# The mixer's between-chunks product as three fp32r passes of high and low parts, with signed decay sums kept once and their turns two slots later

## What is computed

```
proj = einsum('bsd,ed->bse', x, in_proj_w)          # gate, x part, B and C, dt
A_cum = cumsum(A_dt)                                # decay sums in chunks of 128
Y_diag = einsum('bzlhn,bzshn,bhzls,bzshp->bzlhp', Cc, Bc, L, xch)
decay_states = exp(A_cum[..., -1:] - A_cum)
states = einsum('bzlhn,bhzl,bzlhp->bzhpn', Bc, decay_states, xch)
Y_off = einsum('bzlhn,bzhpn,bhzl->bzlhp', Cc, prev, exp(A_cum))
Y = Y_diag + Y_off + hs * D
```

## Time and profile before

| | |
|---|---|
| median of 3 runs | 2562.69 us (2562.52 to 2564.77) |
| the profiled execution | 2562.39 us |
| its span, first to last instruction | 2560.7 us |
| busy: PE, PEld | 2473.7 us (97%), 2009.8 us (78%) |
| busy: DVE, ACT, POOL | 1827.8 us (71%), 1486.1 us (58%), 1540.6 us (60%) |
| mean granted TensorE clock | 0.990 |
| the chain that ended last | PE 56%, DVE 2%, POOL 1%, issue 1% |

### The profile page before, as it was taken

One profiled execution on the slowest core, in us unless ns is written; L12 is line 12 of the kernel. 1 busy time (PEld: TensorE's weight loads), 2 busy tenths in 40 slices (PEclk: granted clock), 3 DMA queues, 4 the chain that ended last, 5 costly groups with the idle time before them and its releaser, 6 DMA issues.

```text
span 2560.7 us, 53900 instructions
## 1 busy us (share of the span) xinstructions
PE 2473.7 (97%) x19326; PEld 2009.8 (78%) x19326; DVE 1827.8 (71%) x2688; ACT 1486.1 (58%) x3410; POOL 1540.6 (60%) x1495
## 2 busy tenths in 40 slices
PE   5999999999999888999999999999999999999989
PEld 4878788788887677787888788778878877887777
DVE  5776766767767778668778678587687786785864
ACT  3535535445354465666765775676667657756721
POOL 1654656546556332667767677686677676676810
PEclk8999999999999989999999999999999999999999
DMA  3230230312303024323322222222232223222111
GB/s 101 43 84 29 69 79 22 83 43 49 82 26 71 29 74 160 115 67 115 101 75 83 100 92 75 94 102 96 67 113 94 76 88 104 83 82 94 59 39 49
DMA packets 93549, 199.00 MB, mean 78 GB/s; under 512 B 11248, under 2 KB 19440, under 8 KB 93296
## 3 DMA queue, kind: packets, MB, share of 16 engines
q1 hardware_dynamic: 93296, 195.64, 24.8%
HBM read 184.46 MB, written 11.14 MB: 76 GB/s over the span
## 4 chain that ended last, share of the span: by engine, by line
PE 56%; DVE 2%; POOL 1%; issue 1%; DMA 0%; ACT 0%; SPq 0%; POOLq 0%; DVEq 0%; ACTq 0%
PE proj L210 13%; PE proj L212 12%; PE proj L211 12%; PE core_y L1633 5%; PE core_o L1639 3%; PE turned L245 1%; PE mx_decay L210 1%; PE mx_decay L212 1%; PE mx_decay L211 1%; PE core_y L212 1%; PE core_y L210 1%; PE core_y L211 1%; PE turned L1663 1%; PE mx_normed L1663 1%; PE mx_normed L245 1%; PE core_o L1673 1%
## 5 line engine op out<-in xcount | busy, mean ns | idle before, releaser
L210 PE MATMUL proj<-slab_hi,XTL 128*128 128x512 f32 x816 | 348.3, 427 | 1.0 <-DVE mx_gate L1853 0.4
L193 DVE TENSOR_TENSOR slab_lo<-slab_raw,slab_hi 128x512 fp32r<-128x512 f32 (+2 forms) x256 | 239.2, 946 | 118.7 <-ACT slab_hi L184 117.5
L212 PE MATMUL proj<-slab_hi,XTH 128*128 128x512 f32 x816 | 320.0, 392 | 0.0
L211 PE MATMUL proj<-slab_lo,XTH 128*128 128x512 f32 x816 | 319.0, 391 | 0.0
L210 PE MATMUL proj<-XTH,slab_lo 128*128 128x512 f32 x716 | 289.9, 405 | 25.0 <-PEq L81 7.4
L212 PE MATMUL proj<-XTH,slab_hi 128*128 128x512 f32 x716 | 282.6, 395 | 0.0
L211 PE MATMUL proj<-XTL,slab_hi 128*128 128x512 f32 x716 | 282.4, 394 | 0.0
L210 PE MATMUL proj<-slab_hi,mx_otl 128*128 128x512 f32 x576 | 240.5, 418 | 3.0 <-DVE mx_otl L259 3.0
L1921 POOL TENSOR_TENSOR mx_gate<-mx_gate,mx_hd 128x512 f32<-128x512 f32 x128 | 167.4, 1308 | 102.7 <-DVE mx_hd L1824 91.9
L904 POOL TENSOR_TENSOR at_ropeA<-at_ropeA,at_ropeB 128x512 f32<-128x512 f32 x80 | 110.5, 1381 | 195.0 <-DVE at_ropeB L840 195.0
L212 PE MATMUL proj<-slab_hi,mx_oth 128*128 128x512 f32 x576 | 227.7, 395 | 0.0
(11 more groups left out here) (415 smaller groups left out, 6672.7 us busy)
## 6 DMA issues: line engine op xcount, KB each, us to landing
mx_g_all<-sums SPq DMA_DIRECT2D x128, 512.0 KB, 3.7
at_g_all<-sums SPq DMA_DIRECT2D x64, 256.0 KB, 8.1
slab_raw<-in_w_gate SPq DMA_DIRECT2D x64, 256.0 KB, 2.9
slab_raw<-in_w_out SPq DMA_DIRECT2D x64, 256.0 KB, 2.8
slab_raw<-in_w_x SPq DMA_DIRECT2D x60, 256.0 KB, 4.7
slab_raw<-in_w_q SPq DMA_DIRECT2D x32, 256.0 KB, 2.8
slab_raw<-in_w_g SPq DMA_DIRECT2D x32, 256.0 KB, 2.9
slab_raw<-in_w_o SPq DMA_DIRECT2D x32, 256.0 KB, 5.3
```

The source lines that it names most:

```text
L193: op = nc.vector.tensor_tensor(K.SL[par][:, c, 0:width], K.RAW[c][:, 0:width], hi, ALU.subtract)
L210: nc.tensor.matmul(to[:, 0:bh.shape[-1]], al, bh, start=(c == 0), stop=False)
L211: nc.tensor.matmul(to[:, 0:bh.shape[-1]], ah, bl, start=False, stop=False)
L212: mm = nc.tensor.matmul(to[:, 0:bh.shape[-1]], ah, bh, start=False, stop=(c == KC - 1))
```

## The change

It has four parts.

1. The between-chunks product is made like the units: CBO is kept as a high part (ScalarE's copy at slot 8 of even halves, as before, but rounded) and a low part (VectorE, new), XD as a high part (ScalarE, new) and a low part (VectorE, new), and TensorE does low by high, high by low and high by high in fp32r. The new operations on XD stand in slots r = 1, 4, 8 and 10 (`XD_AT`), after that slot's decays and before its gate. TensorE waits for the low part (`mx_xdl`) where it waited for GpSimd's XD. There is one XD and one low part, where XD had two buffers; GpSimd's next XD waits for the low part of the last.
2. The decay sums are kept once, negated for the first four tiles and as they are for the last four; from_start is made in two operations instead of one.
3. The turns of G and of RR, and the copies out of them, stand at slots 24 and 28 of the middle phase instead of 22 and 26.
4. The small tensors of the last router lie in a free part of another tensor; its operations are the same.

```diff
@@ -923,12 +923,10 @@
     S = K.S
     av, vv, tt, xs = (S[f"{n}_1"] for n in ("rt_a", "rt_v", "rt_T", "rt_x"))
     N, U = K.slab, K.unit
-    def sb(name, shape, dt=F32):
-        return mem.enter_context(nc.sbuf_tensor(f"rt1_{name}", shape, dt))
     scT = room[:, 0:2, :].rearrange("p t n -> p (t n)")
     LG, E, R1, R2 = (room[:, 2 + i, :].rearrange("p (t e) -> p t e", t=NT) for i in range(4))
-    top, top2 = sb("top", [P, NT, 8]), sb("top2", [P, NT, 8])
-    se, rs, ws = sb("sum", [P, NT]), sb("rsum", [P, NT]), sb("wsum", [P, NT])
+    top, top2 = (room[:, 7, i * NT * 8:(i + 1) * NT * 8].rearrange("p (t k) -> p t k", t=NT) for i in range(2))
+    se, rs, ws = (room[:, 7, (16 + i) * NT:(17 + i) * NT] for i in range(3))
     banks = [K.PT, K.PO]
 
     @block.sync
@@ -1081,7 +1079,7 @@
     STEPS = 9
     DT_READY, G_READY, R_READY = 8, 10, 11
     first_block = INTER // P
-    SCAN_AT, Q_AT, G_AT, R_AT, STORE_AT = 14, 18, 22, 26, 15
+    SCAN_AT, Q_AT, G_AT, R_AT, STORE_AT = 14, 18, 24, 28, 15
 
     @block.sync
     def _(sp):
@@ -1359,13 +1357,14 @@
                 for i, bank in enumerate((K.PT, K.PD)):
                     src = bank[:, :].rearrange("p (t h) -> p t h", t=4)
                     act.wait_ge(tt, HEAD + 2 + i + 1)
-                    nc.scalar.activation(less[:, 4 * i:4 * i + 4, :], src, ACT.Copy, scale=-1.0)
-                    nc.scalar.activation(upto[:, 4 * i:4 * i + 4, :], src, ACT.Copy).then_inc(cc, 1)
+                    nc.scalar.activation(signed[:, 4 * i:4 * i + 4, :], src, ACT.Copy, scale=2.0 * i - 1.0).then_inc(cc, 1)
             if u == R_AT:
                 act.wait_ge(tt, HEAD + 5)
                 nc.scalar.activation(to_end[:, :, :].rearrange("p b h -> p (b h)"), K.PT[:, :], ACT.Exp, scale=-1.0).then_inc(cc, 1)
                 act.wait_ge(cc, HEAD + 4)
-                nc.scalar.activation(from_start[:, :, :], upto[:, 1::2, :], ACT.Exp).then_inc(cc, 1)
+                for i in range(2):
+                    nc.scalar.activation(from_start[:, 2 * i:2 * i + 2, :], signed[:, 4 * i + 1:4 * i + 4:2, :], ACT.Exp,
+                                         scale=2.0 * i - 1.0).then_inc(cc, 1)
 
     @block.vector
     def _(dve):
@@ -1519,6 +1518,7 @@
     S = K.S
     N, U, T = K.slab, K.unit, K.tile
     SLOTS, OFF = 24, 8
+    XD_AT = [1, 4, 8, 10]
 
     units = [("x", i) for i in range(8)] + GATE_OUT
     split = {2 * c: [(1, c)] for c in range(4)}
@@ -1551,12 +1551,13 @@
         ACC = sb("ACC", [P, NT, HID])
         BT, CT = sb("BT", [P, TOK]), sb("CT", [P, TOK])
         CBM = sb("CBM", [P, NT, P])
-        CBO = sb("CBO", [P, NB, P])
+        CBH, CBL = sb("CBO_hi", [P, NB, P], F32R), sb("CBO_lo", [P, NB, P], F32R)
         acc = [sb(f"acc{i}", [P, HALF]) for i in range(3)]
         th = sb("th", [P, HALF])
         M = [sb(f"m{i}", [P, 4, P]) for i in range(4)]
         XCH = [sb(f"xch{i}", [P, HH1, P1]) for i in range(2)]
-        XD = [sb(f"xd{i}", [P, HH1, P1]) for i in range(2)]
+        XD, XDL = sb("xd", [P, HH1, P1]), sb("xd_lo", [P, HH1, P1], F32R)
+        XDH = [sb(f"xd_hi{i}", [P, HH1, P1], F32R) for i in range(2)]
         TO = sb("to", [P, HW])
         HD = [sb(f"hd{i}", [P, HW]) for i in range(2)]
         acc.append(HD[1])
@@ -1634,9 +1635,13 @@
                                               XCH[t % 2][:, h, :], start=True, stop=True)
                 mm.then_inc(S["mx_y"], 1)
                 if t % 2:
-                    pe.wait_ge(S["mx_xd"], HEAD + NB * q + b + 1)
+                    pe.wait_ge(S["mx_xdl"], HEAD + NB * q + b + 1)
                     pe.wait_ge(S["mx_to"], HEAD + NB * q + b)
-                    nc.tensor.matmul(K.PO[:, :], CBO[:, b, :], XD[b % 2][:, :, :], start=True, stop=True).then_inc(S["mx_pof"], 1)
+                    if b == 0:
+                        pe.wait_ge(S["mx_cbl"], HEAD + q // 2 + 1)
+                    nc.tensor.matmul(K.PO[:, :], CBL[:, b, :], XDH[b % 2][:, :, :], start=True, stop=False)
+                    nc.tensor.matmul(K.PO[:, :], CBH[:, b, :], XDL[:, :, :], start=False, stop=False)
+                    nc.tensor.matmul(K.PO[:, :], CBH[:, b, :], XDH[b % 2][:, :, :], start=False, stop=True).then_inc(S["mx_pof"], 1)
 
             def half(g, s, last):
                 q = 2 * g + s
@@ -1742,7 +1747,7 @@
                                              TB[u % 2][:, :].rearrange("p (t n) -> p t n", t=4), ACT.Copy).then_inc(S["mx_hs"], 1)
                     if s == 0 and sl == 8:
                         act.wait_ge(S["mx_a"], HEAD + 3 * g + 3)
-                        nc.scalar.activation(CBO[:, :, :].rearrange("p b n -> p (b n)"), K.PO[:, :], ACT.Copy).then_inc(S["mx_bt"], 1)
+                        nc.scalar.activation(CBH[:, :, :].rearrange("p b n -> p (b n)"), K.PO[:, :], ACT.Copy).then_inc(S["mx_bt"], 1)
                     if r in SCORE1:
                         t = SCORE1.index(r)
                         if t < 4:
@@ -1757,14 +1762,19 @@
                             for h in range(4):
                                 at, head = PD[k][:, h * P:(h + 1) * P], ds(HH1 * q + 4 * k + h, 1)
                                 if t < 4:
-                                    ex = nc.scalar.activation(at, GB[t % 4][:, 4 * k + h, :], ACT.Exp, bias=less[:, t, head])
+                                    ex = nc.scalar.activation(at, GB[t % 4][:, 4 * k + h, :], ACT.Exp, bias=signed[:, t, head])
                                 else:
-                                    rl = nc.scalar.activation(at, GB[t % 4][:, 4 * k + h, :], ACT.Relu, bias=upto[:, t, head], scale=-1.0)
+                                    rl = nc.scalar.activation(at, GB[t % 4][:, 4 * k + h, :], ACT.Relu, bias=signed[:, t, head], scale=-1.0)
                             if t >= 4:
                                 rl.then_inc(S["mx_rl"], 1)
                                 act.wait_ge(S["mx_rl"], HEAD + 8 * q + 2 * (t - 4) + k + 1)
                                 ex = nc.scalar.activation(PD[k][:, :], PD[k][:, :], ACT.Exp, scale=-1.0)
                             ex.then_inc(S["mx_e"], 1)
+                    if r in XD_AT:
+                        b = XD_AT.index(r)
+                        act.wait_ge(S["mx_xd"], HEAD + NB * q + b + 1)
+                        act.wait_ge(S["mx_pof"], HEAD + NB * q + b - 1)
+                        nc.scalar.activation(XDH[b % 2][:, :, :], XD[:, :, :], ACT.Copy).then_inc(S["mx_xdh"], 1)
                     if last and s == 1:
                         for t in XT_AT.get(sl, ()):
                             tile_xt_hi(nc, K, act, "d", t, XTB[t])
@@ -1829,6 +1839,10 @@
                                 dve.wait_ge(S["mx_cm"], HEAD + NT * (q + 1))
                             nc.vector.tensor_tensor(TO[:, :].rearrange("p (h n) -> p h n", h=HH1), K.PO[:, :].rearrange("p (h n) -> p h n", h=HH1),
                                                     bc(from_start[:, b, ds(HH1 * q, HH1)], [P, HH1, P1]), ALU.mult).then_inc(S["mx_to"], 1)
+                    if s == 0 and sl == 8:
+                        dve.wait_ge(S["mx_bt"], HEAD + g + 1)
+                        nc.vector.tensor_tensor(CBL[:, :, :].rearrange("p b n -> p (b n)"), K.PO[:, :],
+                                                CBH[:, :, :].rearrange("p b n -> p (b n)").bitcast(F32), ALU.subtract).then_inc(S["mx_cbl"], 1)
                     if r in SCORE1:
                         t = SCORE1.index(r)
                         for k in range(2):
@@ -1845,6 +1859,11 @@
                         dve.wait_ge(S["mx_cm"], HEAD + NT * q + sl - 1)
                         a = acc[(sl - 1) % 4][:, :]
                         nc.vector.scalar_tensor_tensor(a, TH[(sl - 1) % 2][:, :], 1.0, a, ALU.add, ALU.mult).then_inc(S["mx_cm"], 1)
+                    if r in XD_AT:
+                        b = XD_AT.index(r)
+                        dve.wait_ge(S["mx_xdh"], HEAD + NB * q + b + 1)
+                        dve.wait_ge(S["mx_pof"], HEAD + NB * q + b)
+                        nc.vector.tensor_tensor(XDL[:, :, :], XD[:, :, :], XDH[b % 2][:, :, :].bitcast(F32), ALU.subtract).then_inc(S["mx_xdl"], 1)
                     if last and s == 1:
                         for t in XT_AT.get(sl, ()):
                             tile_xt_lo(nc, K, dve, "d", t, XTB[t])
@@ -1938,9 +1957,9 @@
                         hs = HS[:, t, :].rearrange("p (h n) -> p h n", h=HH1)
                         if t % 2 == 0:
                             pool.wait_ge(S["mx_xc"], HEAD + NT * q + t + 1)
-                            pool.wait_ge(S["mx_pof"], HEAD + NB * q + b - 1)
+                            pool.wait_ge(S["mx_xdl"], HEAD + NB * q + b)
                             alone(pool)
-                            nc.gpsimd.tensor_tensor(XD[b % 2][:, :, :], XCH[t % 2][:, :, :], bc(to_end[:, b, heads], [P, HH1, P1]),
+                            nc.gpsimd.tensor_tensor(XD[:, :, :], XCH[t % 2][:, :, :], bc(to_end[:, b, heads], [P, HH1, P1]),
```

12 lines of the change are left out of this document (6 added, 6 removed).

## The result

The changed kernel takes 2568.14 us (median of 20 runs, 2562.57 to 2574.02), the kernel before 2563.72 us beside it: ratio 1.0017, 95% interval 1.001 to 1.0023. A second series gave 1.0011 (1.0002 to 1.002). It is slower by some 3 to 4.4 us; neither interval holds 1. In the series of the experiments two executions lay far off all others (9113 us, one of run 1, and 3080 us, one of the kernel before) and are left out of every ratio. The profiled execution took 2571.65 us with a span of 2569.6.

A forecast was written before the change was run, and what follows sets the result against it. TensorE was taken to bound the mixer, idling only 3.4 us there. Terms -10.9 + 15.8 + 0.5 + 0.9 - 1.1 = +5.2 us on the profiled 2562.4 gave 2567.6, stated as 2567.5 us, range 2557 to 2577.

The forecast's parts named there:

- What the passes give back: Mixer's between-chunks products: three fp32r passes make each 0.17 us shorter, 64 in all, 10.9 us.
- Rival 3: Mixer: the three passes are no shorter, 10.9 us lost but 8.2 us less waiting; 2570 us, slower; chance 0.05.
- The wait at t = 7 for yb(6): Mixer: TensorE's product waits for VectorE's late yb(6), 0.91 us in even and 1.06 in odd halves, 15.8 us.
- about 0.25 of that comes back: Even halves, slot r = 11: VectorE regains 0.25 us at the slab's first low part, leaving yb(6) 0.67 us late.
- so it slips in between at 1185.33 to 1185.93: Odd halves: VectorE's new subtraction fits between two GpSimd operations, taking 0.60 us; yb(6) comes 0.55 us late.
- the second rival: Mixer: the r = 10 subtraction waits out a whole GpSimd operation, 1.30 us; 2577 to 2585 us, slower; chance 0.13.
- Rival 1: Mixer: VectorE makes up the time and no wait arises; 2551 us, faster; chance 0.13.
- Middle phase: VectorE's waits for ScalarE fall from 1.09 to about 0.6 and 2.10 to about 1.65 us; 1.1 us less.
- Rival 4: Middle phase: TensorE's 3.60 us wait was on the path, gain about 4.9 us; 2563.7 us, no change; chance 0.07.
- First group: Mixer's first group: CBO's low part delays the products of t = 0, adding 0.5 us.
- Tail: After the mixer's last half: one more VectorE subtraction and the later copy add about 0.9 us.

The follow-up runs named there:

- run 1: The changed kernel with VectorE doing yb(6) ahead of slot r = 11's slab_lo and otl: ratio 0.9984 to the kernel before, mixer 1365.9 us.
- run 5: The changed kernel with yb(6) first in slot r = 11 and yb(7), TO(3) first in slot r = 12 on VectorE: ratio 0.9974, 2557.2 us.
- run 10: run 5 plus, in odd halves but the last, VectorE's scalings X(3) and X(4) moved to the ends of slots r = 14 and 15: ratio 0.9942, 2549.5 us.
- third order: VectorE's order of run 10: mixer 1363.3 us with the fp32 product and no split, 1353.0 us with the split and three passes.
- run 4: The changed kernel with the mixer's between-chunks product in fp32 as before, keeping the middle-phase changes: ratio 0.9989, middle phase 46.68 us.
- run 3: The changed kernel with the fourth sequence's XD low-part subtraction done on 1 of 64 columns per head: ratio 0.9991, mixer 1367.2 us.
- run 7: The one-column subtraction of run 3 on the changed kernel, with its second operand from PSUM instead of SBUF: ratio 0.9991, mixer 1367.1 us.
- run 11: The kernel before (fp32 product, no split) with VectorE's order of run 10: ratio 0.9977, 2558.8 us.

## Why the prediction was right, and where its steps were off

The forecast was 2567.5 us, 4.9 us over before (against the median); measured are 4.4 and 3.7. The mechanism was right: the passes are shorter by what was forecast, and the wait at t = 7 for yb(6) eats the gain; runs 1, 5 and 10 take that wait away, and the gain comes through as the order on VectorE improves. That the total came so close is in part luck, since four terms were off and partly cancel: the forecast had the even halves 8 x 0.44 = 3.5 us too high, the odd halves 8 x 0.26 = 2.1 and the tail 1.7 too low, and the middle phase's gain 0.5 too large. Point by point:

- **What the passes give back**: 2.52 us forecast from L1634 to the second L210, 2.53 measured, and 0.50 us less from t = 0 to t = 7 wherever nothing waits (runs 1, 5 and 10: 41.46 against 41.96), 3 x 0.17. The 10.3 us between the first and the last column in the third order are nearly the whole 10.9. Rival 3 falls. The Trainium skill (FP8 and Floating Point Precision, TensorE Precision Notes) counts four passes in a true fp32 product; the estimate from that, 0.215 us a product and 13.8 us in all, was too much, as 0.16 to 0.18 was measured.
- **The wait at t = 7 for yb(6)**: the place, the partner and the number of 16 are as forecast. The sum of the mixer was -10.9 + 15.8 + 0.5 = +5.4, measured +4.5. Its two sizes were off against each other. *Even halves*: 0.91 forecast. The turn ahead of the product starts at 1281.29, and the product stands 0.53 behind such a turn when nothing holds it (1278.79 to 1279.32 before), so of 1.08 us 0.55 are the wait. Even halves came out 0.2 us shorter than before, where my terms had them 0.23 longer. The failed step is "about 0.25 of that comes back": two low parts of the slab took 0.39 less, since GpSimd's operation had passed, and the subtraction was not held for my 0.2 us. *Odd halves*: 1.06 forecast, 1.30 measured by the same reckoning in half 1, and on the whole half 0.64 us where the terms had 0.38. The failed step is "so it slips in between at 1185.33 to 1185.93". In half 1 it came 0.13 us after GpSimd's sum had begun, did not slip in behind it, and took 1.71 us in place of 0.60. That is the mechanism of the second rival, in part: the low parts behind it gave 0.43 us back (2.21 to 1.78). The rival's price for the odd halves, 1.1 us each on top, was too much by that: they came out 0.26 over the forecast's terms.
- **Rival 1** (VectorE makes up the time) was wrong for this order, and run 10 shows what it takes: three operations moved ahead and two put off.
- **Middle phase**: 1.1 forecast, 0.5 to 0.6 measured (0.5 to 0.9 over all kernels). The 2.10 us at the exponentials became 1.68, as forecast 1.65; the 1.09 became two waits of 0.52 and 0.37 where I had one of 0.6. Rival 4 falls in the trace; run 4's ratio alone would not exclude it. The first product came 0.2 to 0.5 us earlier behind the first of the silus, not about 1 us.
- **First group**: 0.5 forecast. Half 0 took 42.96 from t = 0 to t = 7 instead of 42.38, and group 0 (halves 0 and 1) 1.2 us more than before, where later groups took 0.4 to 0.7 more: 0.5 to 0.8.
- **Tail**: 0.9 forecast, 2.6 and 2.5 measured. The term had VectorE's extra work and not the clock, and the clock is what the windows show. Why the lower level lasted longer in these profiles stays open.

The four stretches add up to 6.7 us in both profiles of the changed kernel against the one of before; the medians differ by 3.7 to 4.4. No run here assigns the rest. What the numbers show is that 2.6 us of the 6.7 are the tail's, that the tail goes with the clock, and that the two profiled executions of the changed kernel had a clock of 0.987 and 0.988, at the low end of its 0.987 to 0.991.

## What to carry to other kernels

Where TensorE has no idle time left, a matmul made shorter is worth what the slowest chain beside it leaves of it: find first the engine whose result each product waits for, and its room, here 0.27 and 0 us. Work added to that engine costs less by its own length than by what stands behind it in its queue; moving yb and TO ahead and two scalings back turned +4.5 us into -14.7 in the mixer. Run the new order on the old kernel too: of the 14.7 us, 4.4 were the order's and not the change's.

## What the hardware showed that I had not expected

- An operation of 128x8 elements on VectorE took 1.18 us with both operands in SBUF, begun 0.13 us after GpSimd's (run 3, half 3), and 0.16 us with one operand in PSUM, begun 0.13 us after it as well (run 7, half 3).
- A hold that is spared is paid by the next operation with both operands in SBUF: 2.07 became 2.39 us for the slab's low parts (runs 3 and 7). In the changed kernel the subtraction took 0.86 us in half 5 and 1.55 in half 7, and both halves took the same time to t = 7 within 0.05 us.
- After the same pause of 3.3 us behind the mixer TensorE had a mean clock of 1.00 in run 11, of 0.83 over 10 us in the kernel before, and of 0.66 and then 0.83 over 20 us in the changed one, both times it was profiled. The tail took 131.7, 132.9 and 135.5 us. A difference of 1 to 4 us between two single profiles can be this alone.
